# Experts and gates projected ahead of queries and keys, x turned behind them, and one turned bank copied by VectorE in every quarter

## What is computed

```
x = x + 0.5 * ffn(layernorm(x))     # softmax attention with 16 heads of 64, top-2 of 8 experts per head and token
x = x + attn(layernorm(x))          # linear attention, 16 heads of 8, two key/value sets
x = x + 0.5 * ffn(layernorm(x))     # the same ffn, same weights
# inside ffn, for a head h:
q = x @ Wq[h] / 8 ; k = x @ Wk[h]
gate_v, gate_o = x @ Ws[h], x @ Wd[h]         # each picks 2 of 8 experts
v = sum over picked e of sigmoid(gate_v[e]) * (x @ Wv[e])
attn = softmax(q @ k.T) @ v
res = sum over heads and over the experts e picked by gate_o of attn @ Wo[e].T
```

## Time and profile before

| | us |
|---|---|
| median of 3 runs (lowest, highest) | 2408.23 (2405.09, 2417.85) |
| profiled execution, its own time | 2405.05 |
| its span, first to last instruction | 2403.2 |
| PE busy in the span | 2302.7 (96%) |
| DVE, ACT busy | 1991.8 (83%), 1988.5 (83%) |
| POOL busy; DMA engines, mean of q1 | 1148.0 (48%); 55.2% |

### The profile page before, as it was taken

How to read it: one execution, slowest core, us unless ns; L and a number is a source line. 1 busy time by engine, 2 the same in 40 slices (tenths; PEclk the granted TensorE clock), 3 DMA queues, 4 the chain that set the end, 5 groups by cost and what they waited for, 6 DMA issues and landing times.

```text
span 2403.2 us, 120556 instructions
## 1 busy us (share of the span) xinstructions
PE 2302.7 (96%) x49920; PEld 2145.2 (89%) x49920; DVE 1991.8 (83%) x3690; ACT 1988.5 (83%) x6181; POOL 1148.0 (48%) x1126
## 2 busy tenths in 40 slices
PE   3999999999999999999999999999999999999997
PEld 3898888999999999999999999999999999999897
DVE  5887878888888888888888888888888888888884
ACT  3888787888888888888888888888888888888885
POOL 3445555455454454454455454454454554544431
PEclk9999999999999999999999999999999999999999
DMA  4555555555556556556556556556556555556563
GB/s 126 156 169 154 145 152 147 165 165 172 165 162 174 166 163 172 165 159 178 163 162 176 164 152 178 163 161 174 161 158 176 163 167 163 162 160 169 159 174 105
DMA packets 660702, 388.23 MB, mean 162 GB/s; under 512 B 232513, under 2 KB 585665, under 8 KB 660161
## 3 DMA queue, kind: packets, MB, share of 16 engines
q1 hardware_dynamic: 659728, 379.67, 55.2%
q10 hardware_dynamic: 432, 0.85, 0.1%
HBM read 191.64 MB, written 188.74 MB: 158 GB/s over the span
## 4 chain that ended last, share of the span: by engine, by line
PE 84%; ACT 6%; DVE 5%; issue 3%; POOL 1%; DMA 0%; SPq 0%; DVEq 0%; ACTq 0%; POOLq 0%
PE psT L471 18%; PE psS L426 15%; PE psT L488 7%; PE psS L514 7%; PE psT L514 6%; PE psT L490 6%; PE psT L489 6%; PE psT L439 6%; ACT PB L787 5%; PE psT L483 5%; PE psT L453 4%; DVE NMAX L665 1%; DVE QK L731 1%; PE psT L520 1%; PE psT L572 1%
## 5 line engine op out<-in xcount | busy, mean ns | idle before, releaser
L787 ACT ACTIVATE PB<-psS,NMAX 128x256 f32<-128x256 f32 x2048 | 947.2, 497 | 122.6 <-DVE NMAX L665 122.6
L471 PE MATMUL psT<-V,PT 128*64 128x64 f32 x16384 | 538.7, 224 | 8.7 <-issue 8.3
L471 PEld LDWEIGHTS psT<-V,PT 128*64 128x64 f32 x16384 | 501.6, 138 | 35.7 <-issue 10.5
L731 DVE TENSOR_TENSOR QK<-psT,QK 128x512 fp32r<-128x512 f32 x512 | 336.6, 685 | 169.1 <-ACT QK L796 167.1
L787 ACT ACTIVATION_READ_ACCUMULATOR PB<-psS,NMAX 128x1 f32 x2048 | 471.1, 230 | 0.0
L426 PE MATMUL psS<-QK 64*128 64x256 f32 x6144 | 450.3, 288 | 1.5 <-DVE PT L735 1.5
L426 PEld LDWEIGHTS psS<-QK 64*128 64x128 f32 x6144 | 393.9, 187 | 13.9 <-issue 13.7
L665 DVE TENSOR_REDUCE NMAX<-psS 128x2 f32<-128x512 f32 x512 | 329.3, 685 | 86.5 <-PE psS L426 83.2
L796 ACT ACTIVATE QK<-psT 128x512 fp32r<-128x512 f32 x512 | 299.4, 633 | 86.5 <-PE psT L490 73.9
L893 POOL TENSOR_TENSOR BT<-MT,diagv 128x1024 f32<-128x1024 f32 x128 | 305.5, 2387 | 111.5 <-DMA MT<-MIXd 111.5
L899 POOL TENSOR_TENSOR MB<-MASKT,diago 128x1024 f32<-128x1024 f32 x128 | 250.3, 1957 | 142.9 <-DVE GM L738 82.2
(11 more groups left out here) (120 smaller groups left out, 4807.8 us busy)
## 6 DMA issues: line engine op xcount, KB each, us to landing
Vd<-VM SPq DMA_DIRECT2D x512, 128.0 KB, 2.3
V<-Vd SPq DMA_DIRECT2D x512, 128.0 KB, 3.2
AOd<-AO SPq DMA_DIRECT2D x256, 256.0 KB, 2.5
AR<-AOd SPq DMA_DIRECT2D x256, 256.0 KB, 4.2
PJd<-PJ SPq DMA_DIRECT2D x64, 512.0 KB, 2.7
PR<-PJd SPq DMA_DIRECT2D x256, 128.0 KB, 2.7
MIXd<-MIX SPq DMA_DIRECT2D x64, 128.0 KB, 2.2
MT<-MIXd SPq DMA_DIRECT2D x64, 128.0 KB, 2.9
```

Source lines behind the costliest of these rows:

```text
L471: last = eng.matmul(M[64 * u:64 * u + 64, (t * NT + it) * DH:(t * NT + it + 1) * DH], PT[:, t, jt, cols], V[:, pm % 2, 4 * r + t, jt, :], ...
L731: eng.tensor_tensor(QK[:, 1, ab], bank("qk", m).rearrange("p (k t) -> p k t", k=2), QK[:, 0, ab].bitcast(F32), ALU.subtract).then_inc(free ...
L787: eng.activation(PB[:, ab, j, it, :], psS[:, ab, j, it, :], ACT.Exp, bias=NMAX[:, ab, j, it:it + 1], accum_out=SUM[:, p % 2, it, 4 * r + t ...
```

## The change

The order of the items within a quarter changes in three of the four. In r = 0 the expert half comes ahead of queries and keys, in r = 3 the gates do; in r = 2 queries and keys come ahead of the turn of x, `attn_x` and `attn_gram`. ACT's order follows: the expert's or gates' copy stands between the two roundings, which are now two calls; the copies of x and of linear attention stand behind both. DVE copies turned bank 3 in r = 2 as well, and its subtraction for x (`remaining_x`) comes ahead of that copy in even passes and behind it in the others. No instruction is added or removed, and no buffer changes; since banks are taken by place, the item that each one waits for changes too.

```diff
@@ items_of(n), and the same order in the tensor program
                 items += [("expand", p - 1, b) for b in range(2)]
+            if r == 0 and runs(p + 2):
+                items.append(("expert", p + 2, 0))
+            if r == 3 and runs(p + 3):
+                items.append(("gates", p + 3))
+            if works(n + 1):
+                items += [("qk", 2 * n + 2), ("qk", 2 * n + 3)]
             if r == 2:
                 if runs(p + 3):
                     items.append(("xturn", p + 3))
                 if attends(p - 2):
                     items += [("attn_x", p - 2), ("attn_gram", p - 2)]
-            if works(n + 1):
-                items += [("qk", 2 * n + 2), ("qk", 2 * n + 3)]
             if r == 0:
-                if runs(p + 2):
-                    items.append(("expert", p + 2, 0))
...
             if r == 3:
-                if runs(p + 3):
-                    items.append(("gates", p + 3))
@@ vector program
-                if works(n) and r != 2:
+                if r == 2 and runs(p + 3) and attends(p - 2):
+                    remaining_x(p + 3)
+                if works(n):
                     wait_turned(eng, n, 3)
                     wait_full(eng, "product", n - 1)
                     eng.tensor_copy(turned_rows(3), turned(n, 3)...).then_inc(was_copied(n, 3))
+                if r == 2 and runs(p + 3) and not attends(p - 2):
+                    remaining_x(p + 3)
@@ scalar program
+                if works(n + 1):
+                    rounded(n, 0)
+                if r == 0 and runs(p + 2):
+                    copy_expert(p + 2, 0)
+                if r == 3 and runs(p + 3):
+                    ...
+                    eng.activation(GS..., bank("gates", q), ACT.Copy).then_inc(freed("gates", q))
+                if works(n + 1):
+                    rounded(n, 1)
...
-                    for t in (2, 3, 0, 1) if r == 2 else (2, 0, 1):
+                    for t in (2, 0, 1):
```

More of the change, by code:

```diff
@@ L500, in project, with expert @@
                 split_mm(M[:, T:2 * T], lambda c: wk[:, c, i * P:(i + 1) * P], lambda c: XT[:, q % 4, c, :]).then_inc(full("qk", m))
+            def expert(q, i):
+                wait_vacant(eng, "expert", q, i)
+                split_mm(bank("expert", q, i), lambda c: XT[:, q % 4, c, i * P:(i + 1) * P], lambda c: wv[:, c, :]).then_inc(full("expert", q, i))
             def turn(n, ab):
@@ L538, in tensor_program @@
                     expand(p - 1, 1)
+                if r == 0 and runs(p + 2):
+                    expert(p + 2, 0)
+                if r == 3 and runs(p + 3):
+                    q = p + 3
+                    M = bank("gates", q)
+                    wait_vacant(eng, "gates", q)
+                    eng.wait_ge(s_split, 4)
+                    wait_freed(eng, "xturn", q)
+                    for it in range(NT):
+                        last = split_mm(M[:, it * T:(it + 1) * T], lambda c: XT[:, q % 4, c, it * P:(it + 1) * P], lambda c: wg[:, c, :])
+                    last.then_inc(full("gates", q))
+                if works(n + 1):
+                    project(2 * n + 2)
+                    project(2 * n + 3)
                 if r == 2 and runs(p + 3):
@@ L554, in tensor_program @@
                     last.then_inc(full("attn_gram", q))
[L555 to L561, removed]
+                if r == 1 and runs(p + 2):
+                    expert(p + 2, 1)
                 if r == 0 and attends(p - 3):
@@ L587, in tensor_program @@
                     eng.matmul(M[:, C:2 * C], AQ[:, P:2 * P], ST[:, :]).then_inc(full("attn_out", q))
[L588 to L596, removed]
                 if r == 3 and attends(p - 3):
@@ L820, in scalar_program @@
                     exponentials(n, 1)
+                if works(n + 1):
+                    rounded(n, 0)
+                if r == 0 and runs(p + 2):
+                    copy_expert(p + 2, 0)
+                if r == 3 and runs(p + 3):
+                    q = p + 3
+                    wait_full(eng, "gates", q)
+                    if q >= 1:
+                        eng.wait_ge(s_pick, PICKS * (q - 1) + 6)
+                    eng.activation(GS[:, :, :].rearrange("p r e -> p (r e)"), bank("gates", q), ACT.Copy).then_inc(freed("gates", q))
+                if works(n + 1):
+                    rounded(n, 1)
                 if r == 2 and runs(p + 3):
@@ L838, in scalar_program @@
                     eng.activation(GRAM[:, :], bank("attn_gram", q)[:, 0:C + 1], ACT.Copy).then_inc(freed("attn_gram", q))
-                if works(n + 1):
-                    rounded(n)
-                if r in (0, 1) and runs(p + 2):
-                    q = p + 2
-                    wait_full(eng, "expert", q, r)
-                    if q >= 1:
-                        eng.wait_ge(s_pjw, 16 * q)
-                    eng.activation(PJ[:, :, r, :], bank("expert", q, r).rearrange("p (e d) -> p e d", e=E), ACT.Copy).then_inc(freed("expert", q, r))
+                if r == 1 and runs(p + 2):
+                    copy_expert(p + 2, 1)
                 if r == 0 and attends(p - 3):
@@ L858, in scalar_program @@
                     eng.activation(AA[:, :, :].rearrange("p n c -> p (n c)"), bank("attn_out", q)[:, 0:NT * C], ACT.Copy).then_inc(freed("attn_out", q))
-                if r == 3 and runs(p + 3):
-                    q = p + 3
-                    wait_full(eng, "gates", q)
-                    if q >= 1:
-                        eng.wait_ge(s_pick, PICKS * (q - 1) + 6)
-                    eng.activation(GS[:, :, :].rearrange("p r e -> p (r e)"), bank("gates", q), ACT.Copy).then_inc(freed("gates", q))
                 if r == 3 and attends(p - 3):
```

26 lines of the change are left out of this document (15 added, 11 removed).

## The result

| us | before | changed |
|---|---|---|
| median (lowest, highest), 6 runs each | 2413.60 (2405.09, 2418.86) | 2428.79 (2425.26, 2435.83) |
| profiled execution, its own time | 2405.05 | 2426.33 |

What follows compares the result with a forecast made beforehand. PE was taken to bound the kernel (busy 96%), so only its waits could be won. Gains 0.34 + 0.16 + 0.10 + 0.12 less 0.22 made 0.50 us per pair, 12.5 over 25 pairs: 2405.05 to 2392.5, range 2374 to 2412.

Steps and rivals of the forecast that it cites:

- r = 0, even pass: Expert first in r = 0, even passes: psT half's wait goes, scores' second half 0.1 late; gain 0.34 us.
- r = 0, odd pass: Expert first in r = 0, odd passes: attn_q starts earlier, waiting for the expert's bank; gain 0.16 us.
- r = 3: Gates first in r = 3: odd passes gain 0.10 us, DVE's PT taking most back; even passes 0.
- r = 2: Queries and keys first: even passes lose 0.22 us through a new 0.4 wait at attn_gram; odd passes gain 0.12.
- The sum: All quarters of a pair of passes together: 0.50 us gained per pair, 12.5 us over 25 pairs.
- (b): Rival, no change: attn_gram's wait and PT on DVE give gains back; 0.04 us per pair, 2404; chance 0.24.
- The POOL and DMA work behind XN and PJ keeps its order: In r = 2, moving x's turn costs nothing itself; the work behind it keeps its order.
- (a): Rival, more won: neither PT on DVE nor attn_gram holds PE; 1.0 us per pair, 2380; chance 0.13.
- (c): Rival: DVE's steps in the new chains do not overlap; some 0.4 us per pair lost, 2402; chance 0.05.
- (d): Rival, slower: ACT, idle 0.37 us in r = 3, sets the pace there; 0.58 per pair more, 2419.5; chance 0.13.
- The row maximum did leave its 1.0: Sign of error: DVE's row maximum no longer comes its 1.0 us behind the scores.
- the quarters stay as long: Sign of error: PE's waits vanish, yet the quarters get no shorter.

Runs made afterwards that it cites:

- e9: Kernel before with only the r = 0 part (expert ahead of queries and keys, both passes): ratio 0.9996.
- e10: Kernel before with only the r = 3 part (gates ahead of queries and keys): ratio 1.0008.
- e11: Kernel before with only the r = 2 order (queries and keys first; ACT still copies all four turned banks): ratio 1.0088.
- e7: Changed kernel with 16 tiny matmuls (64 PE instructions) at the start: 2407.58 us, ratio 0.9987 to the kernel before.
- e1: As a run (elsewhere the even r = 1 quarter): changed kernel with 32 tiny matmuls (128 PE instructions) at the start: 2425.54 us, ratio 1.0063.
- e13: Changed kernel with 48 tiny matmuls (192 PE instructions) at the start: 2418.63 us, ratio 1.0036 to the kernel before.
- e3: As a run (elsewhere the even r = 3 quarter): changed kernel with PJ's store issued behind the first store of values in r = 2: 2438.58 us, ratio 1.0133.
- e14: Kernel before with gates first in r = 3 and expert first in r = 0 of odd passes only, no shift: 2403.67 us, ratio 0.9974.
- e15: Same as e14 with 64 PE instructions ahead: 2391.65 us, ratio 0.9926 to the kernel before.

## Why the prediction was wrong, step by step

**r = 0, even pass: the steps right, the gain not.** The changed kernel, pass 34, timeline of PE, then ACT, then DVE:

```profile
1320.26 0.50 PE L488 MATMUL psT<-wv,XT 128*128 128x512 f32 x1
...
1323.03 0.72 PE L518 MATMUL psS<-ident,PB 64*128 64x64 f32 x16
1323.58 0.67 PE L518 MATMUL psT<-ident,PB 64*128 64x64 f32 x16
1324.06 1.95 PE L426 MATMUL psS<-QK 64*128 64x256 f32 x24
...
1321.98 0.60 ACT L804 ACTIVATE QK<-psT 128x512 fp32r<-128x512 f32 x1 [0.26 <-PE psT L490]
1322.47 0.59 ACT L817 ACTIVATE PJ<-psT 128x512 f32<-128x512 f32 x1
1322.95 0.61 ACT L804 ACTIVATE QK<-psT 128x512 fp32r<-128x512 f32 x1
...
1322.61 0.69 DVE L736 TENSOR_TENSOR QK<-psT,QK 128x512 fp32r<-128x512 f32 x1 [0.94 <-ACT QK L804]
1323.59 0.69 DVE L736 TENSOR_TENSOR QK<-psT,QK 128x512 fp32r<-128x512 f32 x1 [0.29 <-ACT QK L804]
1324.20 0.68 DVE L742 COPY PT<-psS 128x512 f32<-128x512 f32 x1
```

With T = 1320.26 the first rounding is at T+1.72 (forecast 1.73), PJ at 2.21 (2.22), the second rounding 2.69 (2.71), the subtractions 2.35 and 3.33 (2.38, 3.37), the psT half 0.55 behind the psS half, scores at 3.80 (3.82), PT at 3.94 (3.97). Every step is right to 0.04. What I mis-sized is the stop at the 13th score matmul, behind DVE's PT: it came at T+4.77 (forecast 4.75), but undisturbed it would be 0.80 behind the first and not 0.84, and after a stop the matmul behind it comes 0.20 later instead of 0.12. So 24 scores take 1.95 and not 1.70, 0.25 lost where I had 0.1, and e1 is 0.25 longer. The same stop behind r = 3 is 0.41 and not 0.24 or so. Alone, r = 0 takes 0.46 off e0 (e9), and r = 3 0.34 off o3 without any loss in e0 (e10), because the wait for the psT half's bank, which stood in r = 0 and ended when ACT and DVE were done, took the stop up. In the whole change that wait is gone, and the stop shows in full: e0 is only 0.06 shorter. I had put the stop into r = 3's term, but too small.

**r = 0, odd pass.** Forecast 0.16, measured 0.14 (8.40 to 8.26), alone 0.13. Right.

**r = 3.** Pass 33 of the changed kernel, PE, then ACT (beside the earlier trace rows; T = 1312.58):

```profile
1312.58 0.39 PE L488 MATMUL psT<-wg,XT 128*128 128x256 f32 x1
...
1315.12 0.71 PE L518 MATMUL psS<-ident,PB 64*128 64x64 f32 x16
1315.72 0.71 PE L518 MATMUL psT<-ident,PB 64*128 64x64 f32 x16
1316.21 1.99 PE L426 MATMUL psS<-QK 64*128 64x256 f32 x22
...
1314.30 0.60 ACT L804 ACTIVATE QK<-psT 128x512 fp32r<-128x512 f32 x1
```

The rounding at T+1.72, psT at 3.14 (forecast 3.2), scores at 3.63 (3.7). The quarters of r = 0 and 3 together (e0 -0.06, e1 +0.25, o0 -0.14, and -0.34 of o3) are worth 0.29 per pair, and I had forecast 0.34 + 0.16 + 0.10 = 0.60. The parts alone would add up to 0.66: the missing 0.37 is the stop that the old wait had hidden.

**r = 2: the sum's failed term.** The wait at `attn_gram` is as forecast. Pass 34, r = 2:

```profile
1339.66 0.38 PE L488 MATMUL psT<-XT,wq 128*128 128x256 f32 x1
...
1341.51 0.27 PE L525 MATMUL psT<-ident,AXN 128*128 128x128 f32 x1
1342.05 0.71 PE L571 MATMUL psT<-AXN 128*128 128x129 f32 x4 [0.26 <-DVE QK L736]
1342.69 0.71 PE L518 MATMUL psS<-ident,PB 64*128 64x64 f32 x16
...
1343.72 1.68 PE L426 MATMUL psS<-QK 64*128 64x256 f32 x24
```

`attn_gram` starts at T+2.39 (forecast 2.4), psS at 3.03 (2.95), scores at 4.06 (3.97; 3.51 before). e2 grows by 0.58, o2 by 0.13 (forecast 0.10). Against it I set 0.23 of stop in the scores, in both sorts of pass. In the even one it is there: scores take 1.68, e3 is 0.26 shorter. In the odd one it is not: o3 is 8.57, and 8.61 in e10, which has no change in r = 2, so 0.04 and not 0.22 comes back. r = 2 costs 0.58 - 0.26 + 0.13 - 0.04 = 0.41 per pair where I had 0.22 - 0.12 = 0.10. With ACT's four copies nothing comes back at all (e11: e3 9.10, +0.67 per pair).

**The sum.** r = 0 and 3 0.31 short, r = 2 0.31 over, o1 0.03 less: -0.50 becomes +0.09 per pair. That alone would have given some 2407, in the range and rival (b)'s case ("given back"). Odd r = 0 was right to 0.02. Even r = 0 and r = 3 together came out 0.29 short, even r = 2 cost 0.10 more, odd r = 2 gave 0.21 less: all the same way, since behind each of these quarters something stood close that my sum had put too small.

**The step that was not there.** "The POOL and DMA work behind XN and PJ keeps its order" was true, and I took it to mean that it costs nothing. The sum had no term for the blocks of PE's own program, which share the DMA engines with that work. The other 13 us or so between the medians hang on it, and they make a slower kernel of an almost equal one: a shift of the blocks alone takes them all away (e7). That the place of the blocks decides about 15 to 20 us of the changed kernel is shown by e7 with e1 beside it and, in its middle part, by e13. That each stop is a late block is shown by the block ends of both traces; that the block is late because of a data transfer ahead of it is read from the records at the stops and borne out in one place by e3. Why the new order meets late blocks more often is shown only in part: in odd r = 3 the loads of V are issued 0.44 and not 0.15 ahead of the place, but in even r = 2 PJd<-PJ is issued as long before it as ever. Nor is it shown how the 13 us divide, since every count of stops is of one execution, and the kernel before had 14, 24 and 24 of them at times (2413.60, 2410.83 and 2412.63) that are the same. Also not shown is why a late block's transfer does not get in between two data transfers that leave a gap: for that there is only their order in time. Part of the disturbed time is also not in stops over 0.35 (e14 to e15: 11 us, of which stops 3.7).

**The rivals.** (a) fell with the stops behind r = 0 and 3; (b) is what the schedule did. (c), DVE's steps one after another: no; PT starts 0.61 after the subtraction (1323.59, 1324.20), 0.08 ahead of its end, as in the earlier trace rows. (d) had the sign and not the mechanism: ACT waits more for PE now (L804 151.7 us, 73.9 before), so it does not set the pace. The row maximum did leave its 1.0 in one place, 1.40 behind the scores in r = 0 of even passes (1325.46), which I had named as a sign of error and in the same breath as expected; it costs nothing, since e1's 0.25 is all in the scores' own stop. The last sign, "the quarters stay as long", is the one that came.

## What to carry to other kernels

When several waits on the critical engine are removed, add up only what single-part runs show together: gains that draw on one reserve of another engine do not add. Before costing a reorder at nothing because an engine keeps its order, ask against what the transfers now fall, the engine's own instructions too. And a change of 0.5% in a long unrolled program should be timed at two or three places of the instruction blocks before it is judged: here 64 instructions at the start were worth as much as the change, though in the kernel before they were worth nothing, and the same schedule ran in 2403.7 and in 2391.7.

## What the runs showed that I had not expected

PE's program of 6.55 MB comes over the DMA queues while it runs: 400 transfers of 16,384 bytes for 102,401 instruction records, each 0.9 to 2.3 us long (median about 1.1), one in some 6 us. They share the 16 engines with data. Most start 0.7 to 1.6 us after PE has passed the end of the block before, a few even ahead of it. Where one landed less than 1.0 us before PE reached the next end, or behind it (at the two places read above, behind 512 KB of PJd<-PJ and behind loads of V), PE stood still for up to 1.65 us in the midst of 64 equal matmuls, and went on 1.3 to 1.6 after the landing. The view of waits shows this only as "issue". In the changed kernel 27 such stops held 27.7 us; with 64 more instructions at the start 25 held 19.5, and the kernel was 0.9% faster (2407.58 against 2428.79, two chips; their kernels before 2411.58 and 2413.60).
